# Gram matrices from the blocks on and above the diagonal, in a Trainium2 decoder-block kernel

## The chip, the cores and the metric

The kernel runs on one core of one Trainium2 chip. The metric is the device time of one execution in microseconds (us). Engines are named as in the profile: PE is TensorE's matmuls, PEld its weight loads, DVE is VectorE, ACT is ScalarE, POOL is GpSimd and SP is SyncE, which here only issues DMAs. Each engine works through its own list of instructions in order, and waits on semaphores for the others.

## What is computed

A pre-norm decoder block on x of 4 samples, 512 rows of 512 features: self-attention along the feature axis, a cross-attention with a context, and a gated feed-forward net with ternary weights. The change touches the first of the three. Cut to that:

```python
x = x + attn(layernorm(x), Wq, bq, Wk, bk, Wv, bv, Wo, bo)
# attn: 16 heads
q = (x @ Wq + bq).reshape(B, T, 128, 16)
k = (x @ Wk + bk).reshape(B, T, 128, 16)
v = (x @ Wv + bv).reshape(B, T, 128, 16)
q, k, v = transpose(q, (0, 3, 2, 1)), transpose(k, (0, 3, 1, 2)), transpose(v, (0, 3, 2, 1))
att = softmax(q @ k / sqrt(128))       # 128 x 128 per head: the sum runs over the 512 rows
y = transpose(att @ v, (0, 2, 1, 3)).reshape(B, -1, 2048)
return y @ Wo + bo
```

Since the scores are sums over the rows, they are Wq^T (X^T X) Wk for the normalised X. The kernel therefore makes the 512 x 512 Gram matrix G = X^T X once for each sample. G is symmetric. Biases are folded into the weights with the help of a constant added to one column of X.

## The kernel before

Matmuls run in a split form: each fp32 operand is a high part (fp32r, written by ACT as a copy) and a low part (the rest, a subtraction on DVE or POOL), and `three_passes` (L100) multiplies high by high, high by low and low by high into one PSUM bank. So each 128 x 512 piece of a product takes 3 matmuls for each of 4 contraction chunks: 12 matmuls.

Attention runs in two passes of two samples each (PB = 2). In pass 0 the two Gram matrices come first of all. Those of pass 1 stand at the end of pass 0: in the last of four `pe_values` rounds, `pe_gram(1, 0)` comes ahead of `pe_out` of sample 0, and `pe_gram(1, 1)` ahead of `pe_out` of sample 1 (L1030). After the Gram matrices, `pe_m` forms G Wk (M, with the split weights wah and wal), and it waits at its start for the low parts of both.

A tile of G is 128 rows of it (c = 0 to 3), 512 columns wide, one bank. The path of a tile: PE fills the bank and adds to a_ready; ACT writes the high part gh (`act_high`, adds to a_hi); DVE writes the low part gl from bank minus gh (`dve_low`, adds to a_free). All tiles of attention (G, M, Y, R) share a ring of four banks (RING_A) in one numbering (`attention_tiles`, A), and `pe_bank` makes PE wait only when it comes round to a bank whose tile is not yet freed. So PE can run up to four tiles ahead of ACT and DVE. `pe_gram` before reads only ph and pl, the split input, not gh or gl.

What stands around the Gram tiles on each engine, in this order:

- pass 0, ACT: high parts ph of sample 0; tiles 0 and 1 of sample 0; ph of sample 1; tiles 2 and 3; wah; the tiles of sample 1; wbh.
- pass 0, DVE: normalises sample 0 and writes pl; normalises sample 1 in full; the low parts of sample 0's tiles; the bias into raw_a (`dve_bias`), half of wal (`dve_split_a`); the low parts of sample 1's tiles; the bias into raw_b.
- pass 0, POOL: pl of sample 1, each quarter behind its ph, then the other half of wal.
- pass 1, DVE: the low parts of the last Y tiles, the bias into raw_a, half of wal, the low parts of sample 0's Gram tiles, four `dve_out` (the sums xacc), the bias into raw_b, the low parts of sample 1's Gram tiles.
- pass 1, ACT: ph, wah (waits for all of raw_a), sample 0's Gram tiles, wbh (waits for raw_b), sample 1's Gram tiles.

Of the kernel before, what the change touches and what calls it, by code (L numbers as in the profile page):

```python
# [17 lines left out]
F32 = mybir.dt.float32  # L18
F32R = mybir.dt.float32r
I32 = mybir.dt.int32  # L20
ACT = mybir.ActivationFunctionType
ALU = mybir.AluOpType
AX = mybir.AxisListType.X

P = 128
B, T, C = 4, 512, 512
CK = C // P
TJ = T // P
# [30 lines left out]
    return [k // 3 * 2 + k % 3 for k in range(max(0, SLOTS * j - CK + 1), SLOTS * j + 3 * CK) if k % 3 < 2 and k // 3 * 2 < TERNARY]  # L59


def attention_tiles():

    for i in range(PB):
        for c in range(CK):
            yield "G", 0, i, c
    for p in range(PASSES):
        for g in range(GROUPS):
            for c in range(CK):
                for i in range(PB):  # L70
                    yield "M", p, g, c, i
        for j in range(GROUPS):
            for c in range(CK):
                yield "Y", p, j, 0, c
            for c in range(CK):
                for hp in range(2):
                    yield "R", p, j, c, hp
            for c in range(CK):
                yield "Y", p, j, 1, c
            if j == GROUPS - 1 and p + 1 < PASSES:  # L80
                for i in range(PB):
                    for c in range(CK):
                        yield "G", p + 1, i, c


A = {key: n for n, key in enumerate(attention_tiles())}


# [11 lines left out]
def three_passes(pe, out, wh, wl, xh, xl, start, stop, shared=False):  # L100

    pe.matmul(out, wh, xh, start=start, stop=False, skip_group_check=shared)  # L102
    pe.matmul(out, wh, xl, start=False, stop=False, skip_group_check=shared)  # L103
    return pe.matmul(out, wl, xh, start=False, stop=stop, skip_group_check=shared)  # L104


def decoder_block(nc, x, ctx, wk, wq, wo, wvt, bk, bq, bv_col, bo, gamma, w1t, w3t, w2t, out):
# [7 lines left out]
    with stack:  # L115
# [3 lines left out]
        s = {}  # L119
# [14 lines left out]
        ident = stack.enter_context(nc.sbuf_tensor("ident", [P, P], F32))  # L134
# [31 lines left out]
        def sa(name, shape, dt=F32):  # L166
            return mem_a.enter_context(nc.sbuf_tensor(name, shape, dt))
# [5 lines left out]
        gh, gl = [None] * PB, [None] * PB  # L173
# [6 lines left out]
        ph, pl = sa("ph", [P, PB, TJ, C], F32R), sa("pl", [P, PB, TJ, C], F32R)  # L180
# [16 lines left out]
        def a_bank(u):  # L197
            return bank[u % RING_A]
# [30 lines left out]
        def wait_a(eng, p, step, c):  # L229

            if step < GROUPS and c < 2:
                eng.wait_ge(s["wal_dve"], wal_dve(p, step) + c + 1)
            elif step < GROUPS:
                eng.wait_ge(s["wal_pool"], wal_pool(p, step) + c - 1)
            else:
                eng.wait_ge(s["wal_pool"], wal_pool(p, step) + c + 1)
# [346 lines left out]
        def stage_b_act(act):  # L583
            turns(act.Fori, lambda b, f, nxt: act_turn(act, b, f, nxt))
# [313 lines left out]
        @block.sync  # L898
        def _(sp):
            credit(sp, "sp")  # L900
            gate(sp, "sp")
            for i in range(PB):
                sp_rows_in(sp, 0, i)
            sp_slot_a(sp, 0, 0)
            sp_row(sp, wk, bk, 0)
            sp_slot_b(sp, 0, 0)
            sp.dma_start(bvc[:], bv_col).then_inc(s["bv_in"], 16)
            for w in range(3):
                sp_magnitudes(sp, 0, w)
            sp.wait_ge(s["wadd_a"], wadd_a(0, 1))  # L910
            sp_row(sp, wq, bq, 0)
            for p in range(PASSES):
                sp_scores(sp, p)
                sp_values(sp, p)
            stage_b_sp(sp)


        def pe_bank(pe, u):
            if u >= RING_A:
                pe.wait_ge(s["a_free"], u - RING_A + 1)  # L920

        def pe_gram(pe, p, i):
            for c in range(CK):
                u = A["G", p, i, c]
                pe_bank(pe, u)
                for j in range(TJ):
                    if c == 0:
                        if p == 0 and i == 0:
                            pe.wait_ge(s["pl_dve"], j + 1)
                        else:  # L930
                            pe.wait_ge(s["pl_pool"], TJ * (PB * p + i - 1) + j + 1)
                    mm = three_passes(pe, a_bank(u)[:], ph[:, i, j, c * P:(c + 1) * P], pl[:, i, j, c * P:(c + 1) * P],
                                      ph[:, i, j, :], pl[:, i, j, :], j == 0, j == TJ - 1)
                mm.then_inc(s["a_ready"], 1)

        def pe_m(pe, p, g, c):
            for i in range(PB):
                u = A["M", p, g, c, i]
                pe_bank(pe, u)
                if g == 0 and c == 0:  # L940
                    pe.wait_ge(s["a_free"], A["G", p, i, CK - 1] + 1)
                for k in range(CK):
                    if c == 0 and i == 0:
                        wait_a(pe, p, g, k)
                    mm = three_passes(pe, a_bank(u)[:], gh[i][:, k, c * P:(c + 1) * P], gl[i][:, k, c * P:(c + 1) * P],
                                      wah[:, k, :], wal[:, k, :], k == 0, k == CK - 1)
                mm.then_inc(s["a_ready"], 1)
# [113 lines left out]
        def act_high(act, dst, u):  # L1061
            act.wait_ge(s["a_ready"], u + 1)
            act.activation(dst, a_bank(u)[:], ACT.Copy).then_inc(s["a_hi"], 1)  # L1063

        def act_gram(act, p, i, cs=range(CK)):
            if p and i == 0:
                for w in range(3):
                    act.wait_ge(s[f"w_stored{w}"], 16 * (TERNARY // 3))
            for c in cs:
                act_high(act, gh[i][:, c, :], A["G", p, i, c])  # L1070

        def act_split_a(act, p, step):

# [88 lines left out]
        @block.scalar  # L1162
        def _(act):
            act_rows(act, 0, 0)
            act_gram(act, 0, 0, range(2))
            act_rows(act, 0, 1)
            act_gram(act, 0, 0, range(2, CK))
            act_split_a(act, 0, 0)
            act_gram(act, 0, 1)
            act_split_b(act, 0, 0)  # L1170
            act.wait_ge(s["w_pad"], 1)
            for p in range(PASSES):
                act_scores(act, p)
                act_values(act, p)
            act_prep(act, 0, 0)
            stage_b_act(act)
# [35 lines left out]
        def dve_low(dve, dst, high, u):  # L1212
            dve.wait_ge(s["a_hi"], u + 1)
            dve.tensor_tensor(dst, a_bank(u)[:], high.bitcast(F32), ALU.subtract).then_inc(s["a_free"], 1)  # L1214

        def dve_gram(dve, p, i):
            for c in range(CK):
                dve_low(dve, gl[i][:, c, :], gh[i][:, c, :], A["G", p, i, c])

        def dve_bias(dve, link, p, g, slot):  # L1220

# [80 lines left out]
        def dve_values(dve, link, p):  # L1302
            for j in range(GROUPS):
# [15 lines left out]
                if last and further:  # L1319
                    dve_bias(dve, link, p + 1, 0, "a")  # L1320
                    dve_split_a(dve, p + 1, 0)
                    dve_gram(dve, p + 1, 0)
# [169 lines left out]
```

## Time and profile before

| | us |
|---|---|
| median of three runs | 1224.45 |
| lowest and highest of them | 1220.92, 1225.1 |
| the profiled execution | 1221.23 |
| its span in the trace | 1219.4 |
| PE busy | 1144.5 (94%) |
| DVE busy | 791.8 (65%) |
| ACT busy | 536.4 (44%) |
| POOL busy | 461.5 (38%) |

The span runs from the first to the last instruction of the profiled execution; 1.83 us lie around it. A busy PE counts a matmul until its modelled end, though the next has long started; the distance from start to start tells what a matmul costs in a row of them. The timeline of an engine shows when each instruction starts and for how long it was busy, with the idle time before it and what ended that in brackets.

### The profile page before, as it was taken

How to read it: one execution, taken by the hardware profiler on the slowest of the kernel's cores; microseconds unless marked ns; L12 is line 12 of the kernel's file. 1: busy time of each engine (PE TensorE's matmuls, PEld its weight loads, DVE VectorE, ACT ScalarE, POOL GpSimd, SP SyncE). 2: the span in 40 equal slices, each digit the busy share in tenths (PEclk: the TensorE clock that was granted, in tenths of full speed). 3: DMA queues.
4: the chain of work that ended last, by engine and by line, in shares of the span. 5: the costliest groups of instructions: out<-in, count | busy, mean ns of one | idle time of the engine just before them, and what ended most of it. 6: DMA issues, size and time to landing. Idle time of an engine off the chain costs nothing.

```text
span 1219.4 us, 16711 instructions
## 1 busy us (share of the span) xinstructions
PE 1144.5 (94%) x5856; PEld 952.4 (78%) x5856; DVE 791.8 (65%) x1469; ACT 536.4 (44%) x1129; POOL 461.5 (38%) x392
## 2 busy tenths in 40 slices
PE   4999988999999999899999978779999999999998
PEld 3888876878788888788888856568878887888786
DVE  7566559889465666453452378878867886787531
ACT  2455562314041244441232227657727762875230
POOL 2222249041341133461403026446625651674030
PEclk9999989999999999999999979979999999999999
DMA  6465553555302143312200132921103110310000
GB/s 224 131 186 181 185 173 109 180 175 170 110 19 85 59 156 113 127 55 70 69 1 1 35 129 66 323 70 54 52 21 102 51 35 34 94 46 1 35 1 35
DMA packets 50480, 114.76 MB, mean 94 GB/s; under 512 B 9721, under 2 KB 9721, under 8 KB 48362
## 3 DMA queue, kind: packets, MB, share of 16 engines
q1 hardware_dynamic: 50410, 113.84, 29.0%
q8 instruction: 42, 0.69, 0.2%
q14 instruction: 28, 0.23, 0.1%
HBM read 97.03 MB, written 16.79 MB: 93 GB/s over the span
## 4 chain that ended last, share of the span: by engine, by line
PE 78%; DVE 11%; ACT 4%; issue 3%; POOL 2%; DMA 1%; SPq 0%; POOLq 0%; ACTq 0%; DVEq 0%
PE bank L102 15%; PE bank L103 15%; PE bank L104 15%; PE bank L435 6%; PE bank L434 6%; PE bank L398 4%; PE bank L446 3%; PE bank L447 3%; PE bank L408 2%; PE bank L409 2%; PE bank L420 2%; PE bank L421 2%; POOL wal L1400 1%; DVE wlow L1352 1%; DVE wraw L1354 1%
## 5 line engine op out<-in xcount | busy, mean ns | idle before, releaser
L1063 ACT ACTIVATE yh<-bank 128x512 fp32r<-128x512 f32 x64 | 38.3, 598 | 244.4 <-PE bank L104 244.4
L434 PE MATMUL bank<-x3h,w 128*128 128x512 f32 (+1 forms) x352 | 141.4, 402 | 1.6 <-DVE x3l L678 1.6
L758 POOL TENSOR_SCALAR pe_x<-pe_x,xri,gam 128x512 f32<-128x512 f32 x128 | 100.9, 789 | 106.4 <-DVE xri L613 100.6
L435 PE MATMUL bank<-x3l,w 128*128 128x512 f32 (+1 forms) x352 | 138.9, 395 | 0.0
L1400 POOL TENSOR_TENSOR wal<-raw_a,wah 128x512 fp32r<-128x512 f32 x48 | 67.5, 1437 | 175.1 <-ACT wah L1084 175.1
L102 PE MATMUL bank<-yh,rh 128*128 128x512 f32 x256 | 101.5, 396 | 7.1 <-DVE xacc L1287 7.0
L1405 POOL TENSOR_TENSOR wbl<-raw_b,wbh 128x512 fp32r<-128x512 f32 x64 | 95.0, 1517 | 34.2 <-ACT wbh L1095 34.2
L102 PE MATMUL bank<-wah,ph 128*128 128x512 f32 x256 | 101.6, 397 | 6.6 <-POOL wal L1400 6.6
L609 DVE TENSOR_REDUCE xmx<-bank 128x1 f32<-128x512 f32 x128 | 87.4, 683 | 28.0 <-PE bank L409 26.8
L523 ACT ACTIVATE pe_x<-bank,xmx 128x512 f32<-128x512 f32 x128 | 87.9, 686 | 37.7 <-DVE xmx L609 36.3
L102 PE MATMUL bank<-wah,gh 128*128 128x512 f32 x256 | 101.0, 394 | 1.7 <-POOL wal L1400 0.8
L1214 DVE TENSOR_TENSOR yl<-bank,yh 128x512 fp32r<-128x512 f32 x64 | 44.2, 690 | 88.7 <-ACT yh L1063 88.5
L103 PE MATMUL bank<-wal,ph 128*128 128x512 f32 x256 | 100.8, 394 | 0.0
L104 PE MATMUL bank<-wah,pl 128*128 128x512 f32 x256 | 100.6, 393 | 0.0
L104 PE MATMUL bank<-yh,rl 128*128 128x512 f32 x256 | 100.4, 392 | 0.0
L103 PE MATMUL bank<-yl,rh 128*128 128x512 f32 x256 | 100.3, 392 | 0.0
L103 PE MATMUL bank<-wal,gh 128*128 128x512 f32 x256 | 100.0, 390 | 0.0
L104 PE MATMUL bank<-wah,gl 128*128 128x512 f32 x256 | 99.7, 390 | 0.0
L604 DVE TENSOR_TENSOR pxl<-bank,pxh 128x512 fp32r<-128x512 f32 x128 | 87.5, 687 | 14.3 <-ACT pxh L519 13.6
L1214 DVE TENSOR_TENSOR ml<-bank,mh 128x512 fp32r<-128x512 f32 x64 | 42.9, 687 | 78.0 <-ACT mh L1063 78.0
L519 ACT ACTIVATE pxh<-bank 128x512 fp32r<-128x512 f32 x128 | 75.6, 594 | 34.1 <-PE bank L398 32.9
L1287 DVE TENSOR_TENSOR xacc<-xacc,bank 128x512 f32<-128x512 f32 x64 | 43.9, 685 | 71.4 <-PE bank L104 71.1
(138 smaller groups left out, 2982.9 us busy)
## 6 DMA issues: line engine op xcount, KB each, us to landing
raw_a<-in_wk SPq DMA_DIRECT2D x8, 1024.0 KB, 5.2
raw_b<-in_wq SPq DMA_DIRECT2D x8, 1024.0 KB, 5.3
raw_a<-in_wo SPq DMA_DIRECT2D x8, 1024.0 KB, 5.8
raw_b<-in_wvt SPq DMA_DIRECT2D x8, 1024.0 KB, 4.8
x1d<-x_scratch SPq DMA_DIRECT2D x64, 128.0 KB, 2.7
kd<-in_ctx SPq DMA_DIRECT2D x64, 128.0 KB, 2.8
ternary_scratch<-wraw SPq DMA_DIRECT2D x24, 341.2 KB, 3.0
w<-ternary_scratch SPq DMA_DIRECT2D x2, 2730.0 KB
```

Of the source, the lines that this page charges most:

```text
L102: pe.matmul(out, wh, xh, start=start, stop=False, skip_group_check=shared)
L103: pe.matmul(out, wh, xl, start=False, stop=False, skip_group_check=shared)
L104: return pe.matmul(out, wl, xh, start=False, stop=stop, skip_group_check=shared)
L434: pe.matmul(u_bank[w][0:m, :], lhs, x3h[:, c, :], start=c == 0, stop=False)
L435: mm = pe.matmul(u_bank[w][0:m, :], lhs, x3l[:, c, :], start=False, stop=c == CK - 1)
L523: act.activation(pe_x[:, q, :], s_bank[q % 2][:], ACT.Exp, bias=xmx[:, q:q + 1], accum_out=xrs[:, q:q + 1]).then_inc(s["s_free"], 1)
L604: dve.tensor_tensor(pxl[:, :, q * P:(q + 1) * P], tb, pxh[:, :, q * P:(q + 1) * P].bitcast(F32), ALU.subtract).then_inc(s["t_free"], 1)
L609: dve.reduce_max(xmx[:, q:q + 1], s_bank[q % 2][:], axis=AX, negate=True).then_inc(s["xmx"], 1)
L758: pool.tensor_scalar(pe_x[:, q, :], pe_x[:, q, :], xri[:, q:q + 1], gam[:], ALU.mult, ALU.mult).then_inc(s["xpn"], 1)
L1214: dve.tensor_tensor(dst, a_bank(u)[:], high.bitcast(F32), ALU.subtract).then_inc(s["a_free"], 1)
L1400: pool.tensor_tensor(wal[:, c, :], raw_a[:, c, :], wah[:, c, :].bitcast(F32), ALU.subtract).then_inc(s["wal_pool"], 1)
L1405: pool.tensor_tensor(wbl[:, c, :], raw_b[:, c, :], wbh[:, c, :].bitcast(F32), ALU.subtract).then_inc(s["wbl"], 1)
```

## The change

Tile c of G now holds only the blocks from the diagonal on: 4 - c blocks, so the moving operand is 512, 384, 256 or 128 columns wide. The six blocks under the diagonal come in three further tiles, x, y and z, of two blocks each. For each such block PE transposes the high part of its mirror block, read from gh, and the low part, read from gl, into one bank; ACT copies the two high blocks to gh, and DVE copies the two low blocks to gl. The order of tiles is 0, 1, x, 2, y, 3, z, and before x, y and z PE waits on a_free until DVE has written the low part of tile 0, 1 and 2. `pe_m` waits for z. The ring now has seven Gram tiles for each sample where it had four. POOL and SP have the same instructions in the same order.

```diff
@@ -59,10 +59,16 @@
     return [k // 3 * 2 + k % 3 for k in range(max(0, SLOTS * j - CK + 1), SLOTS * j + 3 * CK) if k % 3 < 2 and k // 3 * 2 < TERNARY]
 
 
+GRAM = (0, 1, "x", 2, "y", 3, "z")
+MIRROR = {"x": ((0, 1), (0, 2)), "y": ((0, 3), (1, 2)), "z": ((1, 3), (2, 3))}
 def attention_tiles():
 
     for i in range(PB):
-        for c in range(CK):
+        for c in GRAM:
             yield "G", 0, i, c
     for p in range(PASSES):
         for g in range(GROUPS):
@@ -79,7 +85,7 @@
                 yield "Y", p, j, 1, c
             if j == GROUPS - 1 and p + 1 < PASSES:
                 for i in range(PB):
-                    for c in range(CK):
+                    for c in GRAM:
                         yield "G", p + 1, i, c
 
 
@@ -920,17 +926,25 @@
                 pe.wait_ge(s["a_free"], u - RING_A + 1)
 
         def pe_gram(pe, p, i):
-            for c in range(CK):
+            for c in GRAM:
                 u = A["G", p, i, c]
                 pe_bank(pe, u)
+                if c in MIRROR:
+                    pe.wait_ge(s["a_free"], A["G", p, i, MIRROR[c][-1][0]] + 1)
+                    for n, (row, col) in enumerate(MIRROR[c]):
+                        cols = slice(col * P, (col + 1) * P)
+                        pe.transpose(a_bank(u)[:, n * P:(n + 1) * P], gh[i][:, row, cols].bitcast(F32), ident[:])
+                        mm = pe.transpose(a_bank(u)[:, (2 + n) * P:(3 + n) * P], gl[i][:, row, cols].bitcast(F32), ident[:])
+                    mm.then_inc(s["a_ready"], 1)
+                    continue
                 for j in range(TJ):
                     if c == 0:
                         if p == 0 and i == 0:
                             pe.wait_ge(s["pl_dve"], j + 1)
                         else:
                             pe.wait_ge(s["pl_pool"], TJ * (PB * p + i - 1) + j + 1)
-                    mm = three_passes(pe, a_bank(u)[:], ph[:, i, j, c * P:(c + 1) * P], pl[:, i, j, c * P:(c + 1) * P],
-                                      ph[:, i, j, :], pl[:, i, j, :], j == 0, j == TJ - 1)
+                    mm = three_passes(pe, a_bank(u)[:, c * P:], ph[:, i, j, c * P:(c + 1) * P], pl[:, i, j, c * P:(c + 1) * P],
+                                      ph[:, i, j, c * P:], pl[:, i, j, c * P:], j == 0, j == TJ - 1)
                 mm.then_inc(s["a_ready"], 1)
 
         def pe_m(pe, p, g, c):
@@ -938,7 +952,7 @@
                 u = A["M", p, g, c, i]
                 pe_bank(pe, u)
                 if g == 0 and c == 0:
-                    pe.wait_ge(s["a_free"], A["G", p, i, CK - 1] + 1)
+                    pe.wait_ge(s["a_free"], A["G", p, i, "z"] + 1)
                 for k in range(CK):
                     if c == 0 and i == 0:
                         wait_a(pe, p, g, k)
@@ -1062,12 +1076,31 @@
             act.wait_ge(s["a_ready"], u + 1)
             act.activation(dst, a_bank(u)[:], ACT.Copy).then_inc(s["a_hi"], 1)
 
-        def act_gram(act, p, i, cs=range(CK)):
+        def mirrored(g, tile):
+            (r0, c0), (r1, c1) = MIRROR[tile]
+            if c0 == c1:
+                return [(slice(0, 2 * P), g[:, c0, r0 * P:(r1 + 1) * P])]
+            if r0 == r1:
+                return [(slice(0, 2 * P), g[:, c0:c1 + 1, r0 * P:(r0 + 1) * P])]
+            return [(slice(0, P), g[:, c0, r0 * P:(r0 + 1) * P]), (slice(P, 2 * P), g[:, c1, r1 * P:(r1 + 1) * P])]
+        def shaped(ap, like):
+            return ap.rearrange("p (a n) -> p a n", n=P) if len(like.shape) == 3 else ap
+        def act_gram(act, p, i, cs=GRAM):
             if p and i == 0:
                 for w in range(3):
                     act.wait_ge(s[f"w_stored{w}"], 16 * (TERNARY // 3))
             for c in cs:
-                act_high(act, gh[i][:, c, :], A["G", p, i, c])
+                u = A["G", p, i, c]
+                act.wait_ge(s["a_ready"], u + 1)
+                if c in MIRROR:
+                    for cols, dst in mirrored(gh[i], c):
+                        a = act.activation(dst, shaped(a_bank(u)[:, cols], dst), ACT.Copy)
+                    a.then_inc(s["a_hi"], 1)
+                else:
+                    act.activation(gh[i][:, c, c * P:], a_bank(u)[:, c * P:], ACT.Copy).then_inc(s["a_hi"], 1)
 
         def act_split_a(act, p, step):
 
@@ -1162,9 +1195,9 @@
         @block.scalar
         def _(act):
             act_rows(act, 0, 0)
-            act_gram(act, 0, 0, range(2))
+            act_gram(act, 0, 0, GRAM[:3])
             act_rows(act, 0, 1)
-            act_gram(act, 0, 0, range(2, CK))
+            act_gram(act, 0, 0, GRAM[3:])
             act_split_a(act, 0, 0)
             act_gram(act, 0, 1)
             act_split_b(act, 0, 0)
@@ -1214,8 +1247,17 @@
             dve.tensor_tensor(dst, a_bank(u)[:], high.bitcast(F32), ALU.subtract).then_inc(s["a_free"], 1)
 
         def dve_gram(dve, p, i):
-            for c in range(CK):
-                dve_low(dve, gl[i][:, c, :], gh[i][:, c, :], A["G", p, i, c])
+            for c in GRAM:
+                u = A["G", p, i, c]
+                dve.wait_ge(s["a_hi"], u + 1)
+                if c in MIRROR:
+                    for cols, dst in mirrored(gl[i], c):
+                        low = slice(2 * P + cols.start, 2 * P + cols.stop)
+                        d = dve.tensor_copy(dst, shaped(a_bank(u)[:, low], dst))
+                    d.then_inc(s["a_free"], 1)
+                else:
+                    dve.tensor_tensor(gl[i][:, c, c * P:], a_bank(u)[:, c * P:], gh[i][:, c, c * P:].bitcast(F32),
+                                      ALU.subtract).then_inc(s["a_free"], 1)
 
         def dve_bias(dve, link, p, g, slot):
 
```

On PE, in the Gram matrix of sample 0 at the very start (ph and pl are the input's parts, gh_0 and gl_0 the result's), before, from the second tile's last matmuls on:

```order
L102 MATMUL bank1<-ph 128x512
L103 MATMUL bank1<-pl,ph 128x512
L104 MATMUL bank1<-ph,pl 128x512
L102 MATMUL bank2<-ph 128x512
L103 MATMUL bank2<-pl,ph 128x512
```

and now, at the same place, with L936 and L937 the transposes:

```order
L108 MATMUL bank1<-ph 128x384
L109 MATMUL bank1<-pl,ph 128x384
L110 MATMUL bank1<-ph,pl 128x384
L936 MATMUL bank2<-ident,gh_0 128x128 [waits s_a_free]
L937 MATMUL bank2<-ident,gl_0 128x128
L936 MATMUL bank2<-ident,gh_0 128x128
L937 MATMUL bank2<-ident,gl_0 128x128
L108 MATMUL bank3<-ph 128x256
L109 MATMUL bank3<-pl,ph 128x256
```

Tile 2 follows tile 1 at once before; now four transposes that read gh_0 and gl_0 stand between them, behind a wait on a_free.

On ACT, from the start of the program: the high parts of sample 0's input, then those of the Gram tiles (gh), those of sample 1's input (ph), and the first weights (wah). Before:

```order
L1059 ACTIVATE ph<-xnf0 128x512 [waits s_xn] x4
L1063 ACTIVATE gh_0<-bank0 128x512 [waits s_a_ready]
L1063 ACTIVATE gh_0<-bank1 128x512 [waits s_a_ready]
L1059 ACTIVATE ph<-xnf1 128x512 [waits s_xn] x4
L1063 ACTIVATE gh_0<-bank2 128x512 [waits s_a_ready]
L1063 ACTIVATE gh_0<-bank3 128x512 [waits s_a_ready]
```

and now:

```order
L1073 ACTIVATE ph<-xnf0 128x512 [waits s_xn] x4
L1103 ACTIVATE gh_0<-bank0 128x512 [waits s_a_ready]
L1103 ACTIVATE gh_0<-bank1 128x384 [waits s_a_ready]
L1100 ACTIVATE gh_0<-bank2 128x2x128 [waits s_a_ready]
L1073 ACTIVATE ph<-xnf1 128x512 [waits s_xn] x4
L1103 ACTIVATE gh_0<-bank3 128x256 [waits s_a_ready]
L1100 ACTIVATE gh_0<-bank0 128x128 [waits s_a_ready]
L1100 ACTIVATE gh_0<-bank0 128x128
L1103 ACTIVATE gh_0<-bank1 128x128 [waits s_a_ready]
L1100 ACTIVATE gh_0<-bank2 128x256 [waits s_a_ready]
L1117 ACTIVATE wah<-raw_a 128x512 [waits s_raw_a,s_wadd_a]
```

The copy of the mirrored tile x now stands ahead of the four ph of sample 1, and the rest of sample 0's tiles is five copies instead of two.

On DVE, at the end of pass 0, around sample 0's first low parts (gl) for pass 1. Before:

```order
L1226 SCALAR_TENSOR_TENSOR rowb<-rowb 128x512 [waits s_raw_a,s_row_in]
L1228 TENSOR_TENSOR raw_a<-raw_a,rowb 128x512 [waits s_link]
L1228 TENSOR_TENSOR raw_a<-raw_a,rowb 128x512 x3
L1242 TENSOR_TENSOR wal<-raw_a,wah 128x512 [waits s_wah] x2
L1214 TENSOR_TENSOR gl_0<-bank0,gh_0 128x512 [waits s_a_hi]
L1214 TENSOR_TENSOR gl_0<-bank1,gh_0 128x512 [waits s_a_hi]
```

and now:

```order
L1270 TENSOR_TENSOR raw_a<-raw_a,rowb 128x512 [waits s_link]
L1270 TENSOR_TENSOR raw_a<-raw_a,rowb 128x512 x3
L1284 TENSOR_TENSOR wal<-raw_a,wah 128x512 [waits s_wah] x2
L1259 TENSOR_TENSOR gl_0<-bank2,gh_0 128x512 [waits s_a_hi]
L1259 TENSOR_TENSOR gl_0<-bank3,gh_0 128x384 [waits s_a_hi]
L1256 CAST gl_0<-bank0 128x2x128 [waits s_a_hi]
L1259 TENSOR_TENSOR gl_0<-bank1,gh_0 128x256 [waits s_a_hi]
L1256 CAST gl_0<-bank2 128x128 [waits s_a_hi]
L1256 CAST gl_0<-bank2 128x128
L1259 TENSOR_TENSOR gl_0<-bank3,gh_0 128x128 [waits s_a_hi]
L1256 CAST gl_0<-bank0 128x256 [waits s_a_hi]
L1329 TENSOR_TENSOR xacc<-xacc,bank6 128x512 [waits s_out_ready]
```

The bias and the weights' low parts stand ahead of the first gl in both; the four subtractions became eight instructions, and xacc is behind all of them.

## Rows read from the trace of the kernel before

**Rows 1.** The page: busy us of PE (share) xinstructions; granted clock in slices

```profile
PE 1144.5 (94%) x5856; PEld 952.4 (78%) x5856; DVE 791.8 (65%) x1469; ACT 536.4 (44%) x1129; POOL 461.5 (38%) x392
...
PEclk9999989999999999999999979979999999999999
```

**Rows 2.** The page: the chain that ended last, by engine

```profile
PE 78%; DVE 11%; ACT 4%; issue 3%; POOL 2%; DMA 1%; SPq 0%; POOLq 0%; ACTq 0%; DVEq 0%
```

**Rows 3.** Timeline (start us, us) of PE, pass 1: gram, pe_out, gram, pe_out

```profile
350.78 0.39 PE L102 MATMUL bank<-ph 128*128 128x512 f32 x1
...
361.66 0.39 PE L102 MATMUL bank<-yh,rh 128*128 128x512 f32 x1
...
372.54 0.39 PE L102 MATMUL bank<-ph 128*128 128x512 f32 x1
...
383.42 0.39 PE L102 MATMUL bank<-yh,rh 128*128 128x512 f32 x1
```

**Rows 4.** Timeline of PE: twelve 256-column matmuls between these starts

```profile
56.67 0.28 PE L102 MATMUL bank<-mh,wbh 128*128 128x256 f32 x1
...
58.10 0.40 PE L102 MATMUL bank<-wah,gh 128*128 128x512 f32 x1
```

**Rows 5.** Timeline of PE: eight fp32 transposes, and what follows

```profile
449.71 1.04 PE L975 MATMUL bank<-ident,pw 128*128 128x128 f32 x8
450.50 0.36 PE L102 MATMUL bank<-mh,wbh 128*128 128x256 f32 x1
```

**Rows 6.** Timeline of PE, pass 0: gram, its first tile of sample 1, M

```profile
15.00 0.77 PE L102 MATMUL bank<-ph 128*128 128x512 f32 x1 [15.00 <-DVE pl L1377]
...
30.49 0.40 PE L104 MATMUL bank<-ph,pl 128*128 128x512 f32 x1
...
38.89 0.39 PE L102 MATMUL bank<-wah,gh 128*128 128x512 f32 x1
```

**Rows 7.** Timeline of DVE, pass 0: low parts of both Gram matrices

```profile
26.31 2.60 DVE L1214 TENSOR_TENSOR gl<-bank,gh 128x512 fp32r<-128x512 f32 x4
...
35.69 0.69 DVE L1214 TENSOR_TENSOR gl<-bank,gh 128x512 fp32r<-128x512 f32 x1 [0.75 <-ACT gh L1063]
```

**Rows 8.** Timeline of ACT and POOL, pass 0: the split of sample 1

```profile
23.71 1.92 ACT L1059 ACTIVATE ph<-xnf 128x512 fp32r<-128x512 f32 x3 [0.96 <-DVE xnf L1210]
...
24.43 5.43 POOL L1395 TENSOR_TENSOR pl<-xnf,ph 128x512 fp32r<-128x512 f32 x4 [22.56 <-ACT ph L1059]
```

**Rows 9.** Timeline of DVE and ACT, pass 1: ahead of the low parts

```profile
352.22 1.80 DVE L1226 SCALAR_TENSOR_TENSOR rowb<-rowb 128x512 f32<-128x512 f32 x1
...
359.75 2.20 ACT L1084 ACTIVATE wah<-raw_a 128x512 fp32r<-128x512 f32 x4 [6.09 <-DVE raw_a L1228]
...
362.46 2.48 DVE L1214 TENSOR_TENSOR gl<-bank,gh 128x512 fp32r<-128x512 f32 x4 [0.75 <-ACT gh L1063]
...
378.85 0.69 DVE L1214 TENSOR_TENSOR gl<-bank,gh 128x512 fp32r<-128x512 f32 x1 [1.19 <-ACT gh L1063]
```

**Rows 10.** Groups by form (busy us, mean ns | idle before): reads of PSUM

```profile
L514 ACT ACTIVATE vts<-bank 128x256 fp32r<-128x256 f32 x32 | 12.2, 382 | 21.3 <-PE bank L386 21.1
...
L1214 DVE TENSOR_TENSOR gl<-bank,gh 128x512 fp32r<-128x512 f32 x16 | 10.4, 688 | 8.2 <-ACT gh L1063 8.1
```

**Rows 11.** Windows: PE, PEld, DVE, ACT, POOL busy; then clock, DMA, GB/s

```profile
158.00:164.80 6.80, 5.72 (x12) 3.67 (x13) 3.13 (x7) 5.13 (x21) 6.80 (x6) 0.50 0.04 7
199.00:202.30 3.30, 3.30 (x9) 2.56 (x9) 3.26 (x3) 0.00 (x0) 3.30 (x3) 0.50 0.52 162
```

**Rows 12.** Timeline of PE at the start of those two stretches

```profile
159.03 0.77 PE L102 MATMUL bank<-wah,ph 128*128 128x512 f32 x1 [3.24 <-POOL wal L1400]
...
160.02 0.63 PE L104 MATMUL bank<-wah,pl 128*128 128x512 f32 x1
160.45 0.63 PE L102 MATMUL bank<-wah,ph 128*128 128x512 f32 x1
...
198.25 0.50 PE L102 MATMUL bank<-yh,rh 128*128 128x512 f32 x1 [2.03 <-DVE xacc L1287]
```

## The prediction

> **What bounds the kernel now.** I read the page's busy times and the chain first: PE is busy for 94% of the span and has 78% of the chain [rows 1, 2], so a microsecond taken from PE's queue is a microsecond gained, as long as PE goes on without a wait. Next come the four places where a Gram matrix is made, in the timeline of PE. In pass 1 they are seamless: one runs from 350.78 to 361.66, pe_out follows, the next runs from 372.54 to 383.42 [rows 3]. Each is 48 matmuls in 10.88 us, 0.227 us from start to start. In pass 0 the two run from 15.00 to 38.89, where M begins [rows 6]. Last I read DVE, ACT and POOL beside them, because the new tiles x, y and z make PE wait for a low part, which PE never did in this place. The reader is to see there how far DVE runs behind PE: it does the first low part of sample 0 at 26.31, when PE has long finished that tile [rows 7], and in pass 1 at 362.46, when PE has finished all four tiles [rows 3, 9]. The ring of four banks hides this lag now.
>
> **What the change takes from PE.** The columns of a Gram matrix fall from four tiles of 512 to 512, 384, 256 and 128. At 512 a matmul costs 0.227 us [rows 3]; at 256, twelve take from 56.67 to 58.10, 0.119 us each [rows 4]; 384 lies between them, 0.173. For fp32r at 128 no row exists. The line through 512 and 256 would give 0.066; at worst a narrow one costs as much as a wide one, 0.227. The nearest row is an fp32 transpose of 128 columns: eight of them hold PE from 449.71 to 450.50, 0.099 each [rows 5]. I take 0.10. So the twelve of each width cost 2.72 + 2.08 + 1.43 + 1.20 = 7.43 us. The twelve transposes add 12 x 0.105 = 1.26 (rounded up for the change of kind on both sides). Sum 8.7 instead of 10.9: PE has 2.2 us less to do for each Gram matrix, 8.8 us for four.
>
> Those eight transposes each show 0.27 us of length, but that is latency; they start 0.1 us apart [rows 5]. The Trainium skill, "TensorE: Matmul & The Clock Gate", section "Part 4: PE-mode transpose", gives about 275 ns for a transpose in a kernel; the trace has the same length but not that spacing, and if 275 ns were the spacing, the change would cost PE 48 x 0.17 = 8 us more. The same page, "Back-to-back issue gap", has some 81 ns for a matmul of 128 columns with its weight load, by which the narrow ones would cost 0.9 us less in all.
>
> **What it adds in pass 0.** Sample 0: tile 0 still ends at about 19.2, tile 1 at 21.3. Tile x then waits for DVE's first low part, which starts at 26.31 and takes 0.69 [rows 7, 10]: it waits to 27.0, 5.7 us. DVE comes no earlier, since it normalises sample 1 first, and nothing of that hangs on PE. Queued behind x on PE are tiles 2, y, 3 and z; behind x's copy on ACT stand the four ph of sample 1. The transposes end at 27.5 and 0.3 later ACT copies 256 columns, 0.38 us [rows 10]: ph starts at 28.2, where it started at 23.71 before [rows 8]. POOL's four pl take 5.43 [rows 8] and end at 34.3 instead of 29.86. Sample 1's tile 0 on PE waits for the last of them: its last matmul starts at 34.8, where it started at 30.49 [rows 6], and tile 1 ends at 37.1.
>
> DVE goes the other way round. Its low part of tile 2 waits for ACT, which is busy with ph to 30.6: it ends at 31.4. Tile z is transposed after that (31.5 to 31.9), ACT copies to 32.6, DVE to 33.0. All four low parts were done at 28.9 before (26.31 + 2.60) [rows 7]. So the bias, wah, the weights' low parts and then sample 1's low parts come 4.2 us later: the first of them started at 35.69 [rows 7], now at 39.9, and ends at 40.6. PE has waited for it since 37.1, 3.5 us. From a first low part on a Gram matrix has 3.9 us left: x 0.42, tile 2 1.43, y 0.42, tile 3 1.20, z 0.42; y and z find their low parts done by then. M starts at 44.5, not 38.89 [rows 6]: **5.6 us later**. POOL's half of wal, 4.2 later too, is done at 41.5 and hidden by this. M's low parts, the bias into raw_b and wbl shift by about as much, so they make no wait of their own.
>
> **What it adds in pass 1.** Sample 0's tiles 0 and 1 end 4.8 us after 350.78, at 355.6. DVE is then in the bias for raw_a (from 352.22), wah follows at 359.75 on ACT, and only behind both comes the first low part, 362.46 to 363.15 [rows 9, 10]. PE waits 7.5 us for it, and with the 3.9 us the matrix ends at 367.1 instead of 361.66: 5.4 us later. Sample 1: pe_out takes 10.9 as before. In the trace the first low part ends at 379.54 [rows 9], 17.9 us after pe_out's start [rows 3]; DVE's and ACT's work between hangs on pe_out and the bias, and keeps that distance. So 367.1 + 17.9 = 385.0. Tiles 0 and 1 end at 382.8, PE waits 2.2 us, and the matrix ends at 388.9, where it ended at 383.42: 5.5 us later, **5.5 us** for the pass. The second wait there eats the 2.2 us of PE work it saves, and no more.
>
> **The clock.** New waits on PE have a second price. After a wait of 3.24 us the granted clock is 0.50 for 6.8 us, and matmuls start 0.43 us apart instead of 0.227; after one of 2.03 us it is 0.50 for 3.3 us [rows 11, 12]. That is the level of 1.2 GHz instead of 2.4. Twelve matmuls run so in the first stretch, 12 x 0.2 = 2.4 us lost; nine at most in the second, 1.8. The change brings waits of 5.7, 3.5, 7.5 and 2.2 us. I charge 2.4 for the second and for the third. The first falls on short work with slack behind it (0 to 2.0: tiles 2, y and 3 at half speed move z, and so DVE's chain), the fourth is near the shorter row (0 to 1.8); I charge neither. Sum 4.8 us, bounds 0 to 8.6. Everything from M on, and stage B, has the same instructions in the same order; I let it follow unchanged.
>
> **The sum.** 1221.23 (the profiled execution, of which 1219.4 is span) + 5.6 + 5.5 + 4.8 = 1237.1. That execution lies 3.2 us under the median of the runs shown and near the lowest of them; I put the forecast at **1238 us**, 1.1% over the median.
>
> **The rivals.** (1) The forecast: waits and lower clock, 1238, chance 0.57. (2) Waits without a lower clock. For it: one wait of 3.24 us is a single case, and the transposes in between may keep PE up. Against it: both long new waits are longer than that one. 1221.2 + 11.1 = 1232, with the narrow matmuls at 0.066 another 1.6 less, 1231. Chance 0.23. (3) Narrow fp32r matmuls cost like wide ones. 12 x 0.127 = 1.5 us for each matrix, 6.1 in all, since tile 3 stands between the wait and the end of the matrix: 1243, or 1247 with the whole clock term. Nothing in the trace excludes it; the halving from 512 to 256 speaks against. Chance 0.12. (4) Part of the delay is swallowed later, by a wait of PE that is not tied to this chain, such as the 3.24 us for POOL's wal at 159.03 [rows 12]. That wait hangs on ACT's and DVE's work of the same round, which shifts along, so I see no anchor in time; 1227, chance 0.05. (5) Faster: the low parts come in time and PE keeps its 8.8 us. It turns at one point: DVE's first low part of a matrix must end before PE is through tiles 0 and 1, 4.8 us from its start. Then 1212. For it only PE's share of the chain; against it the order on DVE, in which the bias and the normalising stand ahead, in all four places. Chance 0.03.
>
> **How the numbers follow.** 0.5%, 6.1 us, is about what a measurement of this kernel can tell from no change. Cases 1 to 3 are slower by more than that (the low end of 2 is close, so I leave 0.02 of it out), case 4 is within it, case 5 is faster: slower 0.90, same 0.07, faster 0.03. The range takes in cases 1 to 3 with their bounds, 1230 to 1246.
>
> **What would show it.** In the trace after: PE idle before the transposes of tile x in all four matrices, about 5.7, 3.5, 7.5 and 2.2 us, released by DVE's gl; M starting near 44.5 to 48; from the start of the first Gram matrix of pass 1 to that of pe_out 16.3 us or more instead of 10.88; granted clock 0.50 behind the second and third wait. PE's matmuls in the Gram groups sum to less than before. It is wrong if those waits are missing or short, if 128 columns start more than 0.15 us apart, or if the time between the end of pass 1's Gram matrices and the end of the kernel changes.

## The result, and the profile after

The changed kernel takes 1238.38 us (median of four runs, 1235.81 to 1239.96) against 1222.68 of the kernel before in the same comparison: 1.012 times as long, interval 1.0091 to 1.0149. The profiled execution of the changed kernel took 1237.43 us with a span of 1235.6, 16.2 us more than before. The mean granted clock over the span is 0.977, before it was 0.983. One line of its page:

```profile
PE 1144.0 (93%) x5904; PEld 955.6 (77%) x5904; DVE 792.8 (64%) x1485; ACT 538.3 (44%) x1145; POOL 461.3 (37%) x392
```

PE busy was 1144.5 us before [rows 1]. A busy sum does not show the saving: a matmul of 128 columns counts 0.27 us of busy time, though the next one starts 0.11 us later. The starts show where the time went. Timeline of PE in the changed kernel: the first Gram matrix and the transposes of tile x of both samples, then M, in pass 0; and gram, x, pe_out, gram, x, pe_out in pass 1:

```profile
14.80 0.76 PE L108 MATMUL bank<-ph 128*128 128x512 f32 x1 [14.80 <-DVE pl L1419]
...
26.05 0.33 PE L936 MATMUL bank<-ident,gh 128*128 128x128 f32 x1 [3.50 <-DVE gl L1259]
...
39.51 0.30 PE L936 MATMUL bank<-ident,gh 128*128 128x128 f32 x1 [2.74 <-DVE gl L1259]
...
43.51 0.48 PE L108 MATMUL bank<-wah,gh 128*128 128x512 f32 x1
...
355.32 0.39 PE L108 MATMUL bank<-ph 128*128 128x512 f32 x1
...
367.77 0.45 PE L936 MATMUL bank<-ident,gh 128*128 128x128 f32 x1 [7.46 <-DVE gl L1259]
...
373.75 0.48 PE L108 MATMUL bank<-yh,rh 128*128 128x512 f32 x1
...
384.77 0.39 PE L108 MATMUL bank<-ph 128*128 128x512 f32 x1
...
391.91 0.30 PE L936 MATMUL bank<-ident,gh 128*128 128x128 f32 x1 [2.15 <-DVE gl L1259]
...
397.47 0.48 PE L108 MATMUL bank<-yh,rh 128*128 128x512 f32 x1
```

Set against [rows 3, 6], by the distances between the starts:

| us | before | changed | difference |
|---|---|---|---|
| pass 0, first Gram matmul to M | 23.89 | 28.71 | +4.8 |
| pass 1, Gram matrix of sample 0 | 10.88 | 18.43 | +7.6 |
| pe_out of sample 0 | 10.88 | 11.02 | +0.1 |
| Gram matrix of sample 1 | 10.88 | 12.70 | +1.8 |
| all else, to the span's end | 1162.9 | 1164.7 | +1.9 |

All four waits in front of tile x are there, 3.50, 2.74, 7.46 and 2.15 us, and each is released by DVE's gl (L1259). The longest one in the chain of the work that ended last, in that window of pass 1 (start us, us, what; waits for issue and pieces under 0.1 us are left out):

```profile
355.26 0.24 PE bank L110
355.52 0.61 ACT yh L1077
356.76 1.81 DVE rowb L1268
358.60 5.61 DVE raw_a L1270 x4
364.76 1.65 ACT wah L1117 x3
366.42 0.49 ACT gh L1103
366.93 0.70 DVE gl L1259
367.77 0.45 PE bank L936
```

The reader sees the order on DVE in it: when PE ends Y and goes on with tiles 0 and 1, DVE takes the last Y tile, then rowb and the four additions into raw_a for 7.4 us, ACT then makes wah, and only then do ACT's gh and DVE's gl of the Gram tile follow, which has lain finished in its bank since about 358. Before, the same chain ran beside PE's matmuls [rows 9].

The record shows one thing more about these 7.4 us. POOL splits the input of sample 1 meanwhile, and where it does not, the same five DVE instructions take 0.68 + 2.50 = 3.2 us (pass 0 of the changed kernel, from 32.72 on, behind the end of POOL's pl at 32.71). POOL in pass 1:

```profile
356.72 6.33 POOL L1437 TENSOR_TENSOR pl<-xnf,ph 128x512 fp32r<-128x512 f32 x4 [5.87 <-ACT ph L1073]
```

In "pass 1, low parts first" below, where these additions run behind POOL's pl, they take 2.50 us again, and POOL's four take 5.05 instead of 6.33. So some 4.2 us of the wait of 7.46 go with DVE and POOL running side by side. No run moves POOL's work alone, so that share was not tested by itself.

### The profile page after: what moved, and what is told of

Same layout as the page of the kernel before. It is cut to its first block, busy times and chain, and to the rows that moved or that the text cites. A ratio compares the mean times of both kernels' runs of the same rounds, so it can differ in the third digit from the quotient of the medians.

```text
span 1235.6 us, 16850 instructions
## 1 busy us (share of the span) xinstructions
PE 1144.0 (93%) x5904; PEld 955.6 (77%) x5904; DVE 792.8 (64%) x1485; ACT 538.3 (44%) x1145; POOL 461.3 (37%) x392
## 4 chain that ended last, share of the span: by engine, by line
PE 76%; DVE 12%; ACT 4%; issue 3%; POOL 2%; DMA 1%; SPq 0%; POOLq 0%; ACTq 0%; DVEq 0%
PE bank L108 15%; PE bank L109 14%; PE bank L110 14%; PE bank L440 6%; PE bank L441 6%; PE bank L404 4%; PE bank L452 3%; PE bank L453 3%; PE bank L414 2%; PE bank L426 2%; PE bank L415 2%; PE bank L427 2%; POOL wal L1442 2%; DVE wraw L1396 1%; DVE wlow L1394 1%
```

## Experiments

Each was compared with the kernel before on the same chip (1221.11 us for the first four described below, 1221.7 for the last three; the changed kernel's comparison is the one above). The texts under each give the interval of the ratio. The first four expectations were reckoned from 1222.7 us for the kernel before. Stage times and spans are in us and come from the one profiled execution of each kernel, by the starts in PE's timeline, as above:

| kernel | ratio | pass 0 to M | gram, sample 0 | pe_out | gram, sample 1 | span |
|---|---|---|---|---|---|---|
| before | 1 | 23.89 | 10.88 | 10.88 | 10.88 | 1219.4 |
| changed | 1.012 | 28.71 | 18.43 | 11.02 | 12.70 | 1235.6 |
| without the wait | 1.0079 | 26.32 | 16.48 | 12.85 | 9.29 | 1227.2 |
| pass 1 alone | 1.0081 | 23.91 | 17.68 | 11.00 | 12.61 | 1227.0 |
| waits alone | 1.0155 | 32.98 | 20.18 | 10.88 | 12.70 | 1236.6 |
| pass 1, low parts first | 0.9975 | 24.28 | 8.81 | 10.97 | 8.81 | 1215.4 |
| mirrored last, low parts first | 0.9961 | 22.73 | 8.80 | 10.99 | 8.80 | 1214.8 |
| before, reordered | 1.0002 | 23.89 | 10.88 | 10.88 | 10.88 | 1219.4 |
| mirrored last | 1.0015 | 25.03 | 14.94 | 11.89 | 8.80 | 1221.3 |

Theory W is that of the prediction: the waits for low parts, with the low clock behind them, are the cost. Theory S: the many small instructions are.

**Without the wait.** From the changed kernel:

```diff
-pe.wait_ge(s["a_free"], A["G", p, i, MIRROR[c][-1][0]] + 1)
-pe.transpose(..., gh[i][:, row, cols].bitcast(F32), ident[:])
-pe.transpose(..., gl[i][:, row, cols].bitcast(F32), ident[:])
+pe.transpose(..., ph[:, i, row, cols].bitcast(F32), ident[:])
+pe.transpose(..., pl[:, i, row, cols].bitcast(F32), ident[:])
```

> The changed kernel with one thing taken away: the 48 transposes read the input's parts ph and pl instead of gh and gl, and PE has no wait on DVE's low part before them. The blocks under the diagonal therefore hold other data; every instruction, its size and its place in the order are the changed kernel's. Theory W (the four waits for a low part, with the low clock behind them, are the cost): the waits of 3.5, 2.7, 7.5 and 2.2 us before tile x go. But the ring has four banks and now seven tiles, so tile y must wait until DVE has freed the bank of tile 0; worked out from the timeline that leaves a wait of 5.7 us in front of y in pass 1, sample 0 (to 363.15), none or little elsewhere in pass 1, and about 1.3 us later in pass 0. Sum some 3 us of delay and 2.4 of low clock over the kernel before: 1228 us, 1224 to 1231. Theory S (the small transposes and narrow matmuls are what costs): nothing much changes, 1236 to 1239.

Measured: 1230.37 us, ratio 1.0079 (1.0052 to 1.0106). The instructions are the same in number, size and place, and 41% of the loss by the medians (9.3 us are left of 15.7), half of it by the spans, is gone, so S falls. The rest stays, because the wait has moved from tile x to tile y. Timeline of PE, the transposes of tile y of sample 0, in pass 0 and in pass 1:

```profile
27.18 0.33 PE L935 MATMUL bank<-ident,ph 128*128 128x128 f32 x1 [2.52 <-DVE gl L1258]
...
364.22 0.47 PE L935 MATMUL bank<-ident,ph 128*128 128x128 f32 x1 [5.53 <-DVE gl L1258]
```

Tile y comes back to the bank of tile 0, four tiles on, and that bank is free only when DVE has written tile 0's low part. With four tiles for each matrix the ring hid DVE's lag; seven tiles in the same ring do not. The explicit wait and the ring wait for the same event. W had 1228 us; the largest part of the difference lies in pe_out behind that wait, which takes 12.85 us instead of 10.88: the granted clock is 0.50 from 362.1 to 372.1, longer than the 2.4 us of loss that W allowed for.

**Pass 1 alone.** Pass 0 gets full tiles again:

```diff
-            for c in GRAM:
+            for c in gram_tiles(p):      # (0, 1, 2, 3) where p is 0
-                    mm = three_passes(pe, a_bank(u)[:, c * P:], ...
+                    mm = three_passes(pe, a_bank(u)[:, first_col(p, c):], ...
```

> The change in pass 1 alone: pass 0 has its four full tiles of 512 columns and no mirrored tile. Theory W: M of pass 0 starts where it did before (38.9 us, the changed kernel had 43.5), and the two Gram matrices of pass 1 cost what they cost in the changed kernel's trace, 9.4 us more than before. 1222.7 + 9.4 = 1232 us, 1230 to 1235. Rival D (part of the loss is in the later stages, not in the Gram matrices, about 2 us by comparing where PE stands in both traces): then up to 2 us more, 1234. If the loss is all in pass 0, 1223.

Measured: 1230.44 us, ratio 1.0081 (1.0053 to 1.0109), 9.3 us over before, where 9.4 were expected; the time itself lies at the lower end of the expected 1230 to 1235, since before was 1221.11 in this comparison. The stages of pass 1 cost 8.7 us more by their starts, M of pass 0 starts as before. The rest of the span is 1.1 us shorter than in the kernel before, where rival D wanted it some 2 us longer: what the changed kernel's trace loses in later stages does not come with this edit.

**Waits alone.** The kernel before, full tiles, no transposes:

```diff
                 pe_bank(pe, u)
+                if c >= 2:
+                    pe.wait_ge(s["a_free"], A["G", p, i, c - 2] + 1)
```

> The kernel before with the waits alone: full tiles, no transposes, but PE waits before tile 2 for DVE's low part of tile 0, and before tile 3 for that of tile 1. Theory W: in pass 0 M starts 7 to 8 us later (the wait at tile 2 ends at 27.0 and 41 us), in pass 1 PE waits 7.0 us to 363.2 and then 1.6 us, all full work behind it; with two stretches of low clock of 2.4 us each 1222.7 + 7.9 + 8.7 + 4.8 = 1244 us, 1239 to 1248, above the changed kernel since nothing is saved. Theory S (the waits are hidden and the small instructions cost): 1222 to 1225.

Measured: 1239.51 us, ratio 1.0155 (1.0126 to 1.0184). That is 18.4 us over before with no small instruction in it, at the lower edge of what W expected (1244, 1239 to 1248) and far from S. Timeline of PE, the matmuls that wait:

```profile
26.79 0.63 PE L102 MATMUL bank<-ph 128*128 128x512 f32 x1 [3.77 <-DVE gl L1216]
...
42.18 0.47 PE L102 MATMUL bank<-ph 128*128 128x512 f32 x1 [2.63 <-DVE gl L1216]
...
370.58 0.76 PE L102 MATMUL bank<-ph 128*128 128x512 f32 x1 [6.87 <-DVE gl L1216]
...
396.31 0.47 PE L102 MATMUL bank<-ph 128*128 128x512 f32 x1 [1.54 <-DVE gl L1216]
```

In pass 1 sample 0's matrix takes 20.18 us, which is 10.88, the wait of 6.87 and 2.4 more: the price in clock that the prediction had charged. Sample 1's takes 12.70, its wait of 1.54 and only 0.3 more.

**Pass 1, low parts first.** From the kernel with the change in pass 1 alone, in short form:

```diff
 # DVE, last pe_values round
-dve_bias(dve, link, p + 1, 0, "a")
-dve_split_a(dve, p + 1, 0)
 dve_gram(dve, p + 1, 0)
 for a in range(HG):
     dve_out(dve, p, j, 0, a)
+    if a == 0: dve_bias(dve, link, p + 1, 0, "a")
+    if a == 2: dve_split_a(dve, p + 1, 0)
-dve_bias(dve, link, p + 1, 0, "b")
 dve_gram(dve, p + 1, 1)
 ...
+dve_bias(dve, link, p + 1, 0, "b")    # behind the last dve_out
 # ACT
-act_split_a; act_gram(0); act_split_b; act_gram(1)
+act_gram(0); act_split_a; act_gram(1); act_split_b
```

> The change in pass 1 alone, and there ACT and DVE do their parts of sample 0's Gram tiles before the bias into raw_a and wah, and sample 1's before the bias into raw_b and wbh (the bias into raw_a stands behind the first xacc, the low parts wal behind the third, the bias into raw_b behind the last). Theory W: each low part is done before PE has finished tile 1 (4.35 us after the start of a Gram matrix against 4.8), no wait is left, and each of the two matrices takes 8.7 us instead of 10.9: 1222.7 - 4.4 = 1218.3 us, 1216 to 1221. Theory S: the order changes nothing, 1230 to 1234 as with pass 1 alone.

Measured: 1218.3 us, ratio 0.9975 (0.9962 to 0.9987): faster than before by 2.8 us by the medians and 4.0 by the spans. W expected 4.4 us less; that its 1218.3 us was met exactly is chance, since W reckoned from 1222.7. No wait is left; each matrix takes 8.81 us. Timeline of PE, the first matmul or transpose of tiles 0, 1, x, 2, y, 3, z and of pe_out, and below it DVE's first low part, which now ends at 355.80, before x starts at 356.31:

```profile
351.48 0.39 PE L117 MATMUL bank<-ph 128*128 128x512 f32 x1
...
354.20 0.33 PE L117 MATMUL bank<-ph 128*128 128x384 f32 x1
...
356.31 0.27 PE L945 MATMUL bank<-ident,gh 128*128 128x128 f32 x1
...
356.66 0.36 PE L117 MATMUL bank<-ph 128*128 128x256 f32 x1
...
358.18 0.27 PE L945 MATMUL bank<-ident,gh 128*128 128x128 f32 x1
...
358.53 0.31 PE L117 MATMUL bank<-ph 128*128 128x128 f32 x1
...
359.91 0.29 PE L945 MATMUL bank<-ident,gh 128*128 128x128 f32 x1
...
360.29 0.48 PE L117 MATMUL bank<-yh,rh 128*128 128x512 f32 x1
```

```profile
355.11 0.69 DVE L1268 TENSOR_TENSOR gl<-bank,gh 128x512 fp32r<-128x512 f32 x1 [2.11 <-ACT gh L1112]
```

**Before, reordered.** The same reordering of ACT and DVE in the kernel before, full tiles in both passes.

> The kernel before with full tiles in both passes, and only the reordering of ACT and DVE in pass 1 that the faster version had. Theory W: PE had no wait there before, so the order alone brings nothing: 1221.1 us, 1219.5 to 1222.5, each Gram matrix 10.9 us. Rival O (the gain of 2.8 us came from the order, not from fewer columns): 1218.3.

Measured: 1221.33 us, ratio 1.0002 (0.9989 to 1.0015), each Gram matrix 10.88 us. So the gain of the run above is not the order's; it is the 4 us of PE work that the order lets through.

**Mirrored last.** From the changed kernel:

```diff
-GRAM = (0, 1, "x", 2, "y", 3, "z")
+GRAM = (0, 1, 2, 3, "x", "y", "z")
-act_gram(act, 0, 0, GRAM[:3])
+act_gram(act, 0, 0, GRAM[:2])
```

> The changed kernel with one thing moved: tiles in the order 0, 1, 2, 3, x, y, z (and in pass 0 sample 1's ph right behind tile 1 on ACT), ACT and DVE otherwise as changed. Same instructions, same waits. Theory W: only where PE stands at the wait matters. Pass 0: pl of sample 1 is no longer held up behind tile x, M starts near 38.6 us. Pass 1: sample 0's tile x waits from 358.2 to 363.2, 5 us instead of 7.5, with 1.3 us of work behind it instead of 3.9: 2.9 us over before, with 0 to 2.4 of low clock; sample 1 has no wait and saves 2.1. 1221.1 - 0.3 + 2.9 - 2.1 + 2.4 = 1224 us, 1221 to 1226. Theory S (small instructions cost): 1235 or more.

Measured: 1224.15 us, ratio 1.0015 (1.0001 to 1.003). Moving the tiles, and with them ACT's ph of sample 1 in pass 0, takes back 1% of the 1.2. Timeline of PE: the transposes of tile x and the start of pe_out in pass 1; then the window 27 to 34, in this kernel and in the next one, which has the same program in pass 0 (busy us of PE, PEld, DVE, ACT, POOL; clock, DMA share, GB/s):

```profile
363.37 0.45 PE L936 MATMUL bank<-ident,gh 128*128 128x128 f32 x1 [4.79 <-DVE gl L1259]
...
365.81 0.78 PE L108 MATMUL bank<-yh,rh 128*128 128x512 f32 x1
```

```profile
27.00:34.00 7.00, 6.64 (x24) 5.83 (x25) 5.48 (x13) 1.93 (x7) 3.02 (x3) 0.56 0.00 0
...
27.00:34.00 7.00, 7.00 (x44) 6.46 (x44) 5.93 (x14) 2.77 (x9) 2.53 (x3) 1.00 0.04 10
```

In pass 0 M starts 25.03 us after the first matmul, 1.1 later than before where I expected 0.3 earlier: the granted clock is 0.56 in that window. In the next kernel it is 1.00 there, and M starts after 22.73 us. Since pass 0 is one and the same program in both, the 2.3 us between them are no effect of an edit: whether a low clock follows this wait (2.31 us here, 2.57 there) differs from one execution to another. Behind the wait of 4.79 in pass 1, pe_out takes 11.89 us instead of 10.88, so there the low clock costs 1.0 in pe_out and up to 1.2 in the transposes ahead of it (2.44 us from 363.37 to 365.81, against 1.25 where nothing waits).

**Mirrored last, low parts first.** Both edits together, the whole change in both passes.

> The whole change, both passes, but with the order of tiles 0, 1, 2, 3, x, y, z, and in pass 1 ACT's and DVE's Gram parts ahead of the biases as in the run before with that order. Theory W: in pass 1 no wait, 4.1 to 4.4 us saved as in that run. In pass 0 the chain DVE, ACT, POOL sets the start of M, not PE: the mirrored tiles of sample 0 fall into PE's idle time before 28.8 us, sample 1's wait for its low part at about 37, M starts within 1 us of the 38.9 us of before. 1221.1 - 4.4 - 0.3 = 1216.5 us, 1215 to 1219. Rival P (PE's work is the bound in pass 0 too): another 4 us less, 1213.

Measured: 1217.24 us, ratio 0.9961 (0.9946 to 0.9976), the fastest of all, 1216.5 expected. Timeline of PE in pass 0: tile x of sample 0, tile x of sample 1, M:

```profile
26.85 0.30 PE L936 MATMUL bank<-ident,gh 128*128 128x128 f32 x1 [2.57 <-DVE gl L1259]
...
36.20 0.30 PE L936 MATMUL bank<-ident,gh 128*128 128x128 f32 x1 [0.24 <-DVE gl L1259]
...
37.48 0.47 PE L108 MATMUL bank<-wah,gh 128*128 128x512 f32 x1
```

M starts 22.73 us after the first Gram matmul, 1.2 less than before, though PE has 4 us less to do: rival P falls, since most of that is not gained, and PE stands at the waits for DVE's low parts instead. The 1.2 us rest on one execution, and the kernel above shows how far that stage moves with the clock. The two kernels that beat the one before differ by less than their intervals.

## Why the prediction was right, point by point

The forecast of 1238 us and its sign held, and so did the mechanism: four waits for DVE's low parts, and a low clock behind some of them. That the total came within 0.4 us was luck, since three terms were off by 1.7 to 3.2 us and nearly cancelled.

- **PE's work.** Forecast 8.7 us for a matrix, measured 8.81 where nothing waits. By the starts of that run, twelve of 384 columns take 2.11 us (2.08 assumed), twelve of 256 1.52 (1.43), twelve of 128 1.38 (1.20), and four transposes 0.35 to 0.38 (0.42). The 128-column matmul, for which I chose 0.10 between 0.066 and 0.227, costs 0.115. Rival 3 (0.227) falls. The spacing of the transposes, 0.1, was right. The 275 ns that the Trainium skill, "TensorE: Matmul & The Clock Gate", section "Part 4: PE-mode transpose", gives for one in a kernel is near its length in this trace (0.27 us), not its cost in a row. The 81 ns of the Trainium skill, "TensorE: Matmul & The Clock Gate", section "Back-to-back issue gap", for a matmul of 128 columns is under the 115 ns that fp32r measured here.
- **The waits.** Forecast 5.7, 3.5, 7.5, 2.2 us; measured 3.50, 2.74, 7.46, 2.15. Those of pass 1 are exact. In pass 0 two things shortened the first. One has nothing to do with the change: tile 0's matmuls start 0.43 us apart to its end, the spacing that goes with a granted clock of 0.50 elsewhere [rows 12] (the windows of this early stretch show no lower clock), so tile 1 starts at 20.06 and not at 19.2. The instructions up to there are those of before, and "pass 1, low parts first", whose pass 0 is that of before, shows the same spacing up to 20.2. The other is that DVE came at 25.31 instead of 26.31, 0.8 us earlier when the earlier start of the whole (14.80, not 15.00) is taken off. Timeline of DVE, the last normalising step in the kernel before, then that step and the first low parts in the changed kernel, and the first step of the bias before and changed:

```profile
24.88 1.33 DVE L1208 TENSOR_SCALAR xnf<-xnf,mvar,rstd 128x512 f32<-128x512 f32 x1
...
24.67 0.54 DVE L1241 TENSOR_SCALAR xnf<-xnf,mvar,rstd 128x512 f32<-128x512 f32 x1
...
25.31 1.15 DVE L1259 TENSOR_TENSOR gl<-bank,gh 128x512 fp32r<-128x512 f32 x2
...
28.83 1.57 DVE L1226 SCALAR_TENSOR_TENSOR rowb<-rowb 128x512 f32<-128x512 f32 x1
...
32.72 0.68 DVE L1268 SCALAR_TENSOR_TENSOR rowb<-rowb 128x512 f32<-128x512 f32 x1
```

The last L1241 takes 0.54 us, where the same step took 1.33 before. Before, POOL's pl ran beside it [rows 8]; now POOL stands still, since tile x's copy holds up ACT's ph. In the runs without the wait and with the mirrored tiles last, where POOL's pl starts before this step, it takes 1.30 us again. The same comes a second time: rowb takes 0.68 us behind POOL's last pl, where it took 1.57 beside it. I had taken DVE's times as fixed, and DVE gained by the very delay that the change makes. The hold-up itself is in ACT's timeline, tile x's copy and then the four ph, 3.3 us later than before [rows 8]:

```profile
26.75 0.38 ACT L1100 ACTIVATE gh<-bank 128x256 fp32r<-128x256 f32 x1 [3.67 <-PE bank L937]
27.02 2.18 ACT L1073 ACTIVATE ph<-xnf 128x512 fp32r<-128x512 f32 x4
```

- **Pass 0 in sum.** Forecast 5.6 us and 2.4 of low clock, measured 4.8. From sample 1's transposes on it went as forecast, 4.0 us to M; they started 0.9 us sooner than forecast, counted from the first matmul, which is what the shorter rowb saves. The low clock fell on the first resumption, not the second: the window 38 to 50 has a granted clock of 1.00 (the last row of the windows below). The charge of 2.4 for the second wait was the largest mistake in the sum. A fixed charge for each wait was wrong in kind, as the two executions of one pass 0 under "mirrored last" show.
- **Pass 1, sample 0.** Forecast 5.4 and 2.4 of clock, 7.8; measured 7.6.
- **Pass 1, sample 1.** Forecast 0.1, with a clock term of 0 to 1.8 that I did not charge; measured 1.8. The wait of 2.15 us did bring a low clock. Windows of the changed kernel behind the first, third and fourth wait, and around and behind the second (busy us of PE, PEld, DVE, ACT, POOL; clock, DMA share, GB/s):

```profile
27.40:30.70 3.30, 3.30 (x18) 3.30 (x17) 1.10 (x4) 2.52 (x7) 2.97 (x3) 0.50 0.00 0
365.00:372.00 7.00, 4.23 (x21) 4.26 (x21) 2.89 (x6) 3.05 (x7) 2.56 (x2) 0.52 0.51 162
392.50:396.00 3.50, 3.50 (x20) 3.50 (x18) 0.85 (x2) 0.91 (x3) 0.99 (x1) 0.51 0.43 129
...
38.00:50.00 12.00, 10.49 (x65) 9.41 (x66) 7.40 (x13) 5.83 (x15) 5.58 (x5) 1.00 0.38 118
```

- **Everything else.** Forecast unchanged, measured +1.9 us. It is -1.1 in the run with pass 1 alone, -3.0 in that with the waits alone and -2.2 in mirrored last, by span less stages. So it does not come with the waits as such. My own sign of being wrong, a change between the end of pass 1's Gram matrices and the end of the kernel, is met in the trace: 838.1 us instead of 836.0, for the same instructions. What differs is the clock. Two windows behind the Gram stages, the kernel before and then the changed one:

```profile
792.90:806.40 13.50, 6.65 (x29) 5.43 (x29) 9.38 (x29) 2.55 (x5) 2.26 (x2) 0.50 0.00 1
...
805.70:822.60 16.90, 9.59 (x35) 7.92 (x36) 11.99 (x35) 5.40 (x11) 2.75 (x3) 0.50 0.04 11
```

All such stretches in that part add up to 31 us before and 38 in the changed kernel. Seven more of them at half the clock can cost up to 3.4 us. Over the nine profiled executions the part takes 834.5 us where they are shortest (24 us, pass 1 alone) and 838.1 where they are longest, with the others between, nearly in that order. The kernel before, reordered, has 34 us of them with no wait added. The executions of the kernel before alone spread from 1218.39 to 1224.39 us in one comparison, so these 2 us are no more than one execution differs from another; whether the change makes them likelier was not tested.

The sum of my errors: 3.2 too much in pass 0, 1.7 and 1.9 too little in the other two. The rival without a lower clock, 1232 us, was wrong in pass 1, as the windows show: over the 8.81 us of an undisturbed matrix and the wait, sample 0's matrix took 2.2 us more and sample 1's 1.7. The faster rival turned on the point I had named: once the first low part of a matrix ends before PE is through tile 1, the gain comes, 4.1 us by the stages in pass 1.

What I missed altogether is the ring. I read it as hiding DVE's lag, and did not see that three more tiles in it would make PE wait for the same low part even without the explicit wait; it did not change this sum, but it is why removing that wait gave back only 41% of the loss.

## What to carry to other kernels

When a producer starts to read its own results back (here PE transposing what ACT and DVE copied out), the work saved counts only if the copies stand early in those engines' queues; look for what is queued ahead of them, and count the buffers in the ring for the tiles added. Put the dependent steps behind all independent ones, and move long independent work on the copying engines behind the copies: here that turned 1.2% slower into 0.4% faster with the same instructions. A short wait on TensorE can cost nearly as much again in clock (1.7 us behind 2.15 in pass 1), and one execution does not tell whether it will.

## What the runs showed that I had not expected

An fp32r matmul of 128 columns is hardly cheaper here than one of 256. Timeline of PE in the changed kernel at the full clock, the first of twelve of 256 columns, the transposes behind them, the first of twelve of 128, and what follows:

```profile
39.90 0.36 PE L108 MATMUL bank<-ph 128*128 128x256 f32 x1
...
41.40 0.27 PE L936 MATMUL bank<-ident,gh 128*128 128x128 f32 x1
...
41.76 0.31 PE L108 MATMUL bank<-ph 128*128 128x128 f32 x1
...
43.13 0.29 PE L936 MATMUL bank<-ident,gh 128*128 128x128 f32 x1
```

1.50 us for twelve at 256 columns (0.125 each), 1.37 at 128 (0.114 each), while 512 cost 0.227 and 384 about 0.176. From 256 to 128 columns the spacing hardly follows the width. So the last tile of the triangle saves nearly nothing over one twice as wide.

Waits of nearly the same length had different prices in clock: 2.15 us brought 3.4 us of low clock in pass 1, 2.74 us in pass 0 brought none. The two executions of one pass 0 under "mirrored last" show that the wait's length does not decide it: low clock behind 2.31 us, none behind 2.57.
